# Two-layer residual convolution on one core: image transfers in 16 strided pieces of large rows, the wrap pair's products behind their tap, the evens' padding one round earlier

## What is computed

```
x = x + relu(conv3x3(gn(x), kern0) + b0)
x = x + relu(conv3x3(gn(x), kern1) + b1)
kern = einsum('lj,lk,li->ijkl', u, w, v)
gn(v): (v - mean) / sqrt(var + 1e-5), mean and var over 256 x 256 x 2 values of a group
```

## Time and profile before

| | |
|---|---|
| median of 3 runs | 6031.8 us (6019.65 to 6040.02) |
| the profiled execution | 6071.61 us |
| its span | 6069.8 us |
| mean granted TensorE clock in it | 0.933 |
| PE, DVE, ACT, POOL busy | 84%, 45%, 36%, 21% |

### The profile page before, as it was taken

One profiled execution on the slowest core, in us unless ns is written; L12 is line 12 of the kernel. 1 busy time (PEld: TensorE's weight loads), 2 busy tenths in 40 slices (PEclk: granted clock), 3 DMA queues, 4 the chain that ended last, 5 costly groups with the idle time before them and its releaser, 6 DMA issues.

```text
span 6069.8 us, 289573 instructions
## 1 busy us (share of the span) xinstructions
PE 5095.9 (84%) x139776; PEld 2869.6 (47%) x139776; DVE 2722.3 (45%) x3148; ACT 2189.6 (36%) x2242; POOL 1261.0 (21%) x1093
## 2 busy tenths in 40 slices
PE   5888888888888888888888888898888888888887
PEld 3444444444444445445444444454444544444444
DVE  4444444444444444444444444444444444444453
ACT  3333333333423334334333333333333333333342
POOL 3121221212212122121121221211212212112120
PEclk9998999999999989999999999999999999999899
DMA  5554445544455445544454455445544454445434
GB/s 87 94 103 89 86 87 98 100 86 86 93 95 98 86 86 99 100 86 86 90 102 93 86 99 98 89 86 98 102 86 86 88 111 87 86 87 108 90 59 86
DMA packets 2100800, 555.70 MB, mean 92 GB/s; under 512 B 2099248, under 2 KB 2099632, under 8 KB 2099632
## 3 DMA queue, kind: packets, MB, share of 16 engines
q1 hardware_dynamic: 2099632, 537.16, 47.2%
HBM read 268.72 MB, written 268.44 MB: 88 GB/s over the span
## 4 chain that ended last, share of the span: by engine, by line
PE 78%; issue 17%; ACT 1%; DMA 0%; DVE 0%; DVEq 0%; ACTq 0%
PE ps_y L331 32%; PE ps_y L283 25%; PE ps_x L311 8%; PE ps_x L356 8%; PE ps_y L291 3%; PE ps_y L288 1%; ACT evens L422 1%; PE ps_x L253 1%; DMA out<-pixels 0%; ACT relu L411 0%; PE ps_x L263 0%; DVE result L516 0%; DVE pixels L531 0%; ACT relu L414 0%; DVE sums L546 0%
## 5 line engine op out<-in xcount | busy, mean ns | idle before, releaser
L331 PE MATMUL ps_y<-odds,scaled 32*32 32x512 f32 x49152 | 2065.3, 671 | 176.5 <-issue 174.0
L283 PE MATMUL ps_y<-evens,scaled 32*32 32x512 f32 x46080 | 1924.3, 604 | 179.6 <-issue 166.2
L331 PEld LDWEIGHTS ps_y<-odds,scaled 32*32 32x32 f32 x49152 | 917.0, 108 | 1067.1 <-issue 693.7
L283 PEld LDWEIGHTS ps_y<-evens,scaled 32*32 32x32 f32 x46080 | 949.9, 103 | 885.2 <-issue 494.3
L519 DVE TENSOR_TENSOR odds<-ps_x,relu 128x2048 f32<-128x2048 f32 x256 | 586.7, 2292 | 1551.6 <-PE ps_x L311 1182.4
L414 ACT ACTIVATE relu<-ps_y,bias 128x2048 f32<-128x2048 f32 x256 | 503.7, 1967 | 2156.0 <-PE ps_y L331 1993.1
L516 DVE TENSOR_TENSOR result<-ps_x,relu 128x2048 f32<-128x2048 f32 x256 | 586.7, 2292 | 1491.1 <-PE ps_x L356 1244.6
L234 POOL TENSOR_TENSOR fold<-fold,evens 128x1024 f32<-128x1024 f32 x384 | 844.1, 2198 | 586.0 <-DVE evens L503 522.5
L411 ACT ACTIVATE relu<-ps_y,bias 128x2048 f32<-128x2048 f32 x256 | 503.6, 1967 | 1238.5 <-PE ps_y L283 1225.9
L311 PE MATMUL ps_x<-evens,constants 32*32 32x512 f32 x16384 | 841.2, 629 | 83.8 <-issue 83.7
L356 PE MATMUL ps_x<-odds,constants 32*32 32x512 f32 x16384 | 848.8, 646 | 67.3 <-issue 65.2
(11 more groups left out here) (46 smaller groups left out, 1520.2 us busy)
## 6 DMA issues: line engine op xcount, KB each, us to landing
raw<-in_x SPq DMA_DIRECT2D x64, 4096.0 KB, 21.8
out<-pixels SPq DMA_DIRECT2D x64, 4096.0 KB, 21.4
parameters<-in_params SPq DMA_DIRECT2D x2, 96.5 KB, 2.0
constants<-in_consts SPq DMA_DIRECT2D x1, 81.0 KB, 2.1
```

Of the source, the lines that this page charges most:

```text
L283: done = nc.tensor.matmul(ps_y[part, r, :], w0[rows, t * Q:(t + 1) * Q], N0[rows, k:k + EACH, i:i + HQ], start=(t == 0), stop=(t == NTAP - 1))
L331: done = nc.tensor.matmul(ps_y[Q * r:Q * (r + 1), q, :], w1[p % 2][Q * q:Q * (q + 1), t * Q:(t + 1) * Q], t1[Q * q:Q * (q + 1), k:k + EACH ...
```

## The change

It has three parts. First, a load or a store becomes 16 DMAs. DMA o takes the partitions o, o + 16, ..., o + 112 (8 of them) with whole rows of 32 KB, and `RUN` is gone. The waits are the same; `IN_DMAS` and `OUT_DMAS` become 16, so DVE waits for all 16. Second, in round 0 of layer 0 the 448-column products stand where the pairs stood, and the 64-column products of a tap come after all other products of the tap, in a new function `wrap_pair`; those with the mean come behind tap 1 in place of tap 0. The first 448-column product now opens the accumulation. Third, `pad_evens` is issued in round 2 of layer 1 (`EVENS_SUM`) and no longer in round 3.

```diff
-RUN = 256
-IN_DMAS, OUT_DMAS = 1, 1
+STRIDE = 16
+IN_DMAS, OUT_DMAS = STRIDE, STRIDE
...
-EVENS_SUM, EVENS_PAD = 2, 3
+EVENS_SUM = 2
...
-                sp.dma_start(raw[:].rearrange("p a x -> p (a x)"), x_rows[p],
-                             max_dma_last_dim=RUN).then_inc(image_in, 16)
+                for o in range(STRIDE):
+                    sp.dma_start(raw[o::STRIDE, :, :].rearrange("p a x -> p (a x)"),
+                                 x_rows[p][o::STRIDE, :]).then_inc(image_in, 16)
...
-                sp.dma_start(out_rows[p], pixels[:].rearrange("p a x -> p (a x)"),
-                             max_dma_last_dim=RUN).then_inc(image_out, 16)
+                for o in range(STRIDE):
+                    sp.dma_start(out_rows[p][o::STRIDE, :],
+                                 pixels[o::STRIDE, :, :].rearrange("p a x -> p (a x)")).then_inc(image_out, 16)
...
+            def wrap_pair(t, side, i):
+                at, part = NTAP + 2 + t, slice(0, Q)
+                for r in range(QUADS):
+                    rows = slice(Q * r, Q * (r + 1))
+                    done = nc.tensor.matmul(ps_y[part, r, 0:HQ], w0[rows, at * Q:(at + 1) * Q],
+                                            N0[rows, side, i:i + HQ],
+                                            start=False, stop=False, skip_group_check=True)
+                if t == 1:
+                    for r in range(QUADS):
+                        rows = slice(Q * r, Q * (r + 1))
+                        done = nc.tensor.matmul(ps_y[part, r, 0:HQ], w0[rows, (NTAP + 1) * Q:(NTAP + 2) * Q],
+                                                center[0][rows, :].to_broadcast([Q, HQ]),
+                                                start=False, stop=False, skip_group_check=True)
+                return done
...
-                                at = NTAP + 2 + t
-                                nc.tensor.matmul(ps_y[part, r, 0:HQ], w0[rows, at * Q:(at + 1) * Q],
-                                                 N0[rows, k, i:i + HQ],
-                                                 start=(t == 0), stop=False, skip_group_check=True)
                                 nc.tensor.matmul(ps_y[part, r, HQ:WIDE], w0[rows, t * Q:(t + 1) * Q],
                                                  N0[rows, k + 1:k + EACH, i:i + HQ],
-                                                 start=False, stop=False, skip_group_check=True)
-                                if t == 0:
-                                    nc.tensor.matmul(ps_y[part, r, 0:HQ], w0[rows, (NTAP + 1) * Q:(NTAP + 2) * Q],
-                                                     center[0][rows, :].to_broadcast([Q, HQ]),
-                                                     start=False, stop=False, skip_group_check=True)
+                                                 start=(t == 0), stop=False, skip_group_check=True)
+                    if f == 0:
+                        done = wrap_pair(t, side, i)
...
-                    if f == EVENS_PAD and p + 1 < IMAGES:
+                    if f == EVENS_SUM and p + 1 < IMAGES:
                         pad_evens(p + 1)
```

## The result

The changed kernel takes 6011.7 us (median of 20 runs) against 6033.5 us of the kernel before (20 runs): ratio 0.9958, 95% interval 0.9943 to 0.9972. It is faster by 22 us, where 660 us were forecast. The profiled execution has a span of 5986.9 us and a mean granted clock of 0.93, as before.

A forecast was written before the change was run, and what follows sets the result against it. TensorE was taken to be bound by its instruction supply while images move. From the profiled 6071.6 us, less 607, 45 and 35, plus 25, came 5410, or 5370 us against the median; range 5220 to 6050.

The forecast's parts named there:

- What bounds the kernel: Rounds where images move: TensorE lacks instruction packets, which wait some 9 us behind the image's 256-byte packets; 10.7 us an image.
- Part 1: Image loads and stores: 16 DMAs in 32 KB rows remove the small packets ahead of instruction packets; 607 us gained.
- The ends: First load and last store, not hidden by other work: -3 to +15 us each, +25 us taken for both.
- Part 2: The evens' padding issued a round earlier, at an image's edge: 0.7 us an image, 45 us gained.
- Part 3: The wrap pair's short products after the tap's others, round 0 of layer 0: 0.55 us an image, 35 us gained.
- A: Image transfers: instruction packets come little or no sooner, 5952 us, chance 0.12; half the stalls left, about 5660, chance 0.12.
- B: Rounds beside each store and load: instruction packets wait behind queued 32 KB rows; some 7070 us or over 9000; chance 0.22.
- C: Stalls go, but VectorE waits for images as a transfer takes over 55 us: over 6900 us; chance within 0.22.

The follow-up runs named there:

- e10: e7 with its transfers cut into 256-byte pieces (8 partitions, four apart): 0.8715 of the kernel before.
- e1: The changed kernel with the transfers of before (one DMA of 256-byte pieces): 0.9816 of the kernel before, 5939 us.
- e7: The changed kernel with each of the 16 transfers' 8 partitions 4 apart in place of 16 apart: 0.8848 of the kernel before.
- e3: The kernel before with the evens' padding one round earlier and nothing else: 0.9879 of the kernel before.
- e2: The kernel before with the 16 transfers alone: 1.0118 of the kernel before, 6119 us.
- e14: The changed kernel with its own sets of partitions (16 apart) in 256-byte pieces: 1.1262 of the kernel before.
- e8: The changed kernel with one transfer of 128 partitions in rows of 32 KB: 0.9209 of the kernel before.

## Why the prediction was wrong

- **What bounds the kernel: right.** An undisturbed image of 82.45 us against a mean of 93.16, and TensorE's instruction packets as what it lacks. e10, with parts 2 and 3, takes 5263 us where e1 takes 5939, and its mean image is the undisturbed one. That the 676 us between them meet the 675 us priced so closely is chance, since e10's ends are some 25 us longer. The "mostly hidden" of the Trainium skill ("Runtime: NRT & Kernel Launch", section "Instruction fetch mechanics") does not hold here: TensorE was idle for 490 us for want of instructions, and 3 us in e10.
- **Part 1: the step that failed** is "32 KB block an engine for some 2.3 us, which fits into the 4.4 us that TensorE has in hand". A row did take 2.5 us, but a packet waits for more than one: 4.1 to 7.0 us in three classes of eight. Nor are 4.4 us free for it: with 1.04 us for the packet and 1.55 us until TensorE goes on, even one row of 2.5 us would not quite have fitted. The prediction had noted that the wait before was already 9 us where a packet's turn is 22 ns, and used it for a rival only. Of the 607 us nothing came: PE idle for want of instructions is 501 us, before 490. Nor was the spacing of the partitions looked at, on which it all hung (e7).
- **The ends**: +25 us taken, some +58 measured. The first load and the last store cost 20 us each; the wait of the last image for the store before it, 19 us more, was not in the sum. SP's further issues, taken as 5.5 us a transfer, make a load's issue last 10 us and a store's 34; in the loop that stayed hidden.
- **Part 2: right**, 0.7 us an image predicted, 0.73 measured in e3's rows, the relu late by 0.41 us where 0.32 was worked out. In the time it was 73 us for 45, with an interval from 58 to 89; what the rest is stays open.
- **Part 3: the right direction, mis-sized.** 0.55 us was the excess over 69 ns a product; 1.57 us came. The 28 extra products then cost 0.92 us in place of the 1.94 at 69 ns each. Either a product of 64 columns takes less than one of 512, or they run beside others; no row here tells which.
- **The rivals.** The case that came is A's, held at 0.12 for little or none of the gain: parts 2 and 3 alone, 5952 us. Measured were 60 us more. Parts 2 and 3 gave some 30 us more than A's 80, and the transfers cost 71 us (e2) to 86 (e1 against the change), 58 of them at the ends. B's mechanism, a packet behind queued rows, fits the waits of three classes in eight. C needed slower transfers and came in e14.

What stays open: how many pieces an engine holds ahead of a packet. Waits of 2 to 3 rows in the change, 3 rows in e7, 4 in e8, and about 100 pieces of 256 bytes in e10, fit no single number of pieces or bytes, and no run here measured the queue itself.

## What to carry to other kernels

A long unrolled program lives on its instruction supply: where an engine is idle for "issue" while images move, compare an undisturbed round with a disturbed one, and divide the instruction queue's packets by the engine's records. Then keep the engines' queues short and the transfers fast: few partitions in a transfer, spaced as in e7 and not 16 apart, in pieces or transfers that hand an engine little at once; and check the DMA share against the rate, which shows how many engines work and how fast. A long wait measured once (9 us) prices a queue better than one packet's turn does.

## What the runs showed of the hardware

- TensorE's instruction packets go in turn over eight places, of which a transfer of 8 partitions meets three, one of 6 partitions one and a little of a second, and one of 5 or 4 none.
- A packet of 16 KB took 1.04 us in the changed kernel, and TensorE went on 1.55 us after its end.
- Eight engines moved 197 GB/s from partitions 4 apart and 105 GB/s from partitions 16 apart; 16 engines 340 GB/s in rows of 32 KB.
- In 256-byte pieces the partitions 16 apart fell to 79 GB/s, where those 4 apart had 145.
- SP needed 34 us to issue 16 stores in the changed kernel and 10 us for 16 loads, in its timeline:

```profile
3061.63 33.96 SPq L183 DMA_DIRECT2D out<-pixels  x16
3099.70 10.02 SPq L177 DMA_DIRECT2D raw<-in_x  x16
```
